# Transformer and state-space layers on one core: the tree layer's preparation moved from step 11 to step 17 of the second attention loop, and four kinds of DVE work in the first loop a step later

## The chip, the cores and the metric

The kernel runs on one core of a Trainium2 chip. The metric is the device time of one execution in microseconds (us), lower is better. Engines are named as in the profile: PE (TensorE), DVE (VectorE), ACT (ScalarE), POOL (GpSimd) and SP (SyncE), which only issues DMAs here.

## The reference

Six layers are applied in turn to x, four batches of 512 tokens by 128 features, each with its own layer norm:

```
x = x + 0.5 * ffn(layernorm(x))      # three decision trees of 16 leaves make q, k, v; full attention
x = x + mha(layernorm(x))            # 16 heads of 8, rotary positions, ALiBi, causal softmax
x = x + 0.5 * ffn(layernorm(x))
x = x + 0.5 * moe(layernorm(x))      # 8 experts, the best 2 of each token, and a shared one
x = x + mamba(layernorm(x))          # convolution, then a scan over 16 states
x = x + 0.5 * moe(layernorm(x))
```

Only the attention layer and the preparation of the tree layer behind it are touched. Their cores:

```
q = rope(x @ wq.T); k = rope(x @ wk.T); v = x @ wv.T          # 16 heads of 8
scores = q @ k.T / sqrt(8) + slope_h * (j - i), causal
out = softmax(scores) @ v @ out_w.T + out_b
...
for _ in range(4):                                            # the path through one tree
    score = xf . node_w[cur] + node_b[cur]; cur = 2*cur + 1 + (score >= 0)
```

## The kernel before

The four batches are worked through as two **pairs**. Within a pair each layer is two **units**, one for each batch (slot 0 and slot 1), so there are 24 units in all. Every engine runs its own program, written out by hand in the order in which it is to work; engines wait for each other by semaphores. Nothing is scheduled by a compiler: what stands behind a waiting instruction on an engine waits too.

A unit begins with a **prologue**: statistics of x ("stats"), the reciprocal root on POOL and three small DVE steps, then the normed rows ("rows"), a transposition on PE ("turn"), the high part on ACT ("high"), the low part on DVE ("low"). For a tree unit the paths follow: a product with the nodes' weights ("first"), then three times a count on PE and a comparison on DVE ("second", "third", "fourth"). For an attention unit four projections on PE and their rotation on DVE follow ("first", "second" for the queries, "k first", "k second" for the keys); the rotated rows are then split into three bf16 parts. ACT copies a part ("q 0" to "q 2", "k 0" to "k 2", line L920), DVE subtracts it (line L1432), which leaves the rest for the next part. The DVE stages of the rests have the names "third", "fourth", "k rest", "k last". When the last part of a side is there, SP writes the parts to DRAM in six DMAs (`head_rows`, L622) and loads them back spread over the heads (`head_rows_in`, L629 for queries, L633 for keys).

The prologue of a unit is **hosted** in the loop of the unit ahead of it, one stage in a step, so that it fills gaps. Tables say which stage falls in which step, for each engine. `stage_at` (L138) reads them, and `HEAD_LAG` says by how many steps the host's counter is shifted: in the attention loop stage number n comes at step n + HEAD_LAG[slot].

The **attention loop** of a unit (`mha`, on every engine) has 32 steps, 8 for each quad of four heads. In a step PE makes the scores of two heads for a tile of keys (L1790, masks L1793 or L1795) and ACT takes the exponentials (L1011); PE needs those of two steps before to go on, since the scores have two places in PSUM. Every other step PE multiplies with the values (L1819). For numerical safety each query row's maximum must be known before its scores are made. That is the work of the **slots**: a small score product on PE (L1858, mask L1860) and a maximum on DVE (L1446). There are 11 slots for a quad. When a quad's slots are done, DVE splits the maxima into parts (L1453 to L1456), PE transposes them (job "turn", L1573 from a_mp), ACT copies them out (L1028), SP writes and reloads them (L721, L725). `HEADS_PLAN` says which of these jobs fall in which step. The slots of the second unit start in step 19 of the first one's loop, behind "turn" 3, and end in step 17 of the second's. Other jobs: "rows" (PE transposes a quad's result from a_o, DVE normalises it: L1411, L1412), "vals" (the values, ACT copy L1034), "ctr" and "out" (the output projection). The jobs share two PSUM banks by turns: PE may start a job only when the job two places before it in the list has been read out of its bank (`bank_free`). In a step an engine does the loop's own work first, then the jobs of that step, and the hosted stage last.

The first unit's loop hosts the prologue of the second attention unit. In steps 4 to 13 fall the splits and the key rotations; their DVE steps are 4, 5, 6, 8, 11 and 12, and ACT copies its parts in steps 4, 5, 6, 11, 12 and 13. The second unit's loop hosts the tree unit's prologue.

The first slot of the second unit needs the keys loaded back (`rows_of_quads`):

```
1823            def rows_of_quads(k, n):
1825                pe.wait_ge(a_fill.sem, a_fill.at(k // 2, 1 if n < 2 else 3))
1826                pe.wait_ge(a_ldq[n].sem, a_ldq[n].at(k, 0))
1827                pe.wait_ge(a_ldk[n].sem, a_ldk[n].at(k, 1))
```

On ACT a part waits for the rest before it, on DVE a rest waits for its part:

```
 914                        act.wait_ge(a_res.sem, a_res.at(k, 2 * side + c - 1))
1431                dve.wait_ge(a_prt.sem, a_prt.at(k, 3 * side + c))
```

Of the kernel before, what the change touches and what calls it, by code (L numbers as in the profile page):

```python
# [51 lines left out]
def heads_plan():  # L52
# [13 lines left out]
    for step in range(2 * NS2):  # L66
# [15 lines left out]
        if step == NS2 + 9:  # L82
# [15 lines left out]
DVE_STAGES = {0: "stats", 2: "rows", 6: "low", 8: "first", 10: "second", 12: "third",  # L98
              14: "fourth", 15: "ranks", 16: "combine", 17: "row"}
# [31 lines left out]
HEAD_PARTS = [f"{side} {c}" for side in "qk" for c in range(3)]  # L131
HEAD_ROTATIONS = ["first", "second", "k first", "k second"]
HEAD_RESIDUALS = ["third", "fourth", "k rest", "k last"]
HEAD_LAG = {0: -6, 1: 11}
KEYS_LATER = 2


def stage_at(table, i, kind, host):  # L138

    if kind == "mha" and table is not POOL_STAGES:  # L140
        for own, ahead in ((DVE_STAGES, HEAD_DVE_STAGES), (ACT_STAGES, HEAD_ACT_STAGES), (PE_STAGES, HEAD_PE_STAGES)):
            if table is own:
                if host == "mha":
                    ahead = {n + KEYS_LATER * (n >= 15): name for n, name in ahead.items()}
                    if table is ACT_STAGES:
                        ahead[3] = "norm"
                return ahead.get(i)
    if host == "mamba" and table is ACT_STAGES:
        return LOOP_ACT_STAGES[kind].get(i)
    if host == "mamba" and kind == "moe" and table is not POOL_STAGES:  # L150
        return {"stats": LOOP_DVE_STAGES, "turn": LOOP_PE_STAGES}[table[min(table)]].get(i)
    if kind == "mamba":
        table = {n: name for n, name in table.items() if name in ("stats", "guess", "rows", "turn", "high", "low")}
    return table.get(i)
# [25 lines left out]
def program(nc, A, out):  # L180
    with ExitStack() as ctx:
# [579 lines left out]
        def _(pool):  # L761
# [31 lines left out]
            def hand_over(u, i):  # L793
                if u + 1 < NU:
                    prologue(u + 1, stage_at(POOL_STAGES, i, UNITS[u + 1][0], UNITS[u][0]))
# [66 lines left out]
        def _(act):  # L862
# [135 lines left out]
            def mha(u, k):  # L998
# [6 lines left out]
                for s_ in range(NS2):  # L1005
# [8 lines left out]
                    for job, x, n in HEADS_PLAN[at]:  # L1014
                        head_job(k - p + x, job, n)
                    if s_ >= HEAD_LAG[p] + 5 and s_ >= 1:
                        hand_over(u, s_ - HEAD_LAG[p])
                if p == 1:
                    heads_out(k - 1, 2 * QUADS - 1)

            def head_job(k, job, n):
                b = job_bank(HEADS_JOBS.index((job, k % 2, n)))
                if job == "turn":
                    act.wait_ge(a_mtr.sem, a_mtr.at(k, n))
                    if n >= 1 or k % 2 == 1:

                        act.wait_ge(a_mwr.sem, a_mwr.at(k, n - 1))
                    a_mok.by(act.activation(a_mT, bank[0:12, b, 0:T // 2].bitcast(BF16), ACT.Copy))  # L1028
                if job == "vals":
                    act.wait_ge(a_vpr.sem, a_vpr.at(k, 0))  # L1030
                    if k % 2 == 1:

                        act.wait_ge(a_vok.sem, a_vok.at(k - 1, 1))
                    a_vst.by(act.activation(flat(a_vs[:]), bank[:, b, :], ACT.Copy))  # L1034
                if job == "ctr":
                    act.wait_ge(a_ctr.sem, a_ctr.at(k, 0))
                    a_cok.by(act.activation(a_o[:], bank[:, b, :], ACT.Copy))
# [73 lines left out]
            def hand_over(u, i):  # L1111
                if u + 1 < NU:
                    prologue(u + 1, stage_at(ACT_STAGES, i, UNITS[u + 1][0], UNITS[u][0]))
# [13 lines left out]
        def _(dve):  # L1127
# [257 lines left out]
            def mha(u, k, p):  # L1385
# [11 lines left out]
                for s_ in range(NS2):  # L1397
                    for job, x, which in HEADS_PLAN[NS2 * p + s_]:
                        head_job(k - p + x, job, which, b - p + x)
                    if s_ >= HEAD_LAG[p] and s_ >= 1:  # L1400
                        hand_over(u, s_ - HEAD_LAG[p])
            def normalise(k, g):

                dve.wait_ge(a_otr.sem, a_otr.at(k, g))
                if g >= 1 or k % 2 == 1:
                    dve.wait_ge(a_norm.sem, a_norm.at(k, g - 1))
                if g == 0 and k % 2 == 1:

                    dve.wait_ge(a_ctr.sem, a_ctr.at(k - 1, 0))
                src = bank[:, job_bank(HEADS_JOBS.index(("rows", k % 2, g))), :].rearrange("p (t c w) -> p t c w", t=NT, c=4)  # L1410
                step(V.reciprocal(a_rec[:], src[:, :, :, DH]))  # L1411
                a_norm.by(V.tensor_tensor(a_rows[:, :, 32 * g:32 * g + 32].rearrange("p t (c d) -> p t c d", d=DH),  # L1412
                                          src[:, :, :, 0:DH], a_rec[:].unsqueeze(3).to_broadcast([P, NT, 4, DH]),
                                          ALU.mult))
# [19 lines left out]
            def head_job(k, job, n, batch):  # L1434
                if job == "rows":
                    normalise(k, n)
                if job == "out":
                    dve.wait_ge(a_out.sem, a_out.at(k, 0))
                    a_fin.by(add_rows(batch, bank[:, job_bank(HEADS_JOBS.index((job, k % 2, n))), :]))
                    dve.wait_ge(a_fin.sem, a_fin.at(k, 0))  # L1440
                if job == "slot":
                    quad, (qt, h0, nh) = n // NS1, SLOTS_4[n % NS1]
                    w = (qt + 1) * P
                    dve.wait_ge(a_s1.sem, a_s1.at(k, n))
                    src = bank[:, job_bank(HEADS_JOBS.index((job, k % 2, n))), 0:nh * w].rearrange("p (h w) -> p h w", w=w)
                    a_m1.by(V.tensor_reduce(a_mx[:, quad, qt, h0:h0 + nh], src, AX_X, ALU.max, negate=True))  # L1446
                    if n % NS1 == NS1 - 1:
                        max_parts(k, quad)
# [96 lines left out]
            def hand_over(u, i):  # L1545
                if u + 1 < NU:
                    prologue(u + 1, stage_at(DVE_STAGES, i, UNITS[u + 1][0], UNITS[u][0]))
# [10 lines left out]
        def _(pe):  # L1558
# [208 lines left out]
            def mha(u, k, p):  # L1767
# [9 lines left out]
                for s_ in range(NS2 + 3 * p):  # L1777
# [23 lines left out]
                    if at >= 3 and at % 2 == 1:  # L1801
                        weigh_heads(k - p, (at - 3) // 2)
                    if s_ > HEAD_LAG[p] and 1 <= s_ < NS2:
                        hand_over(u, s_ - HEAD_LAG[p])
            def weigh_heads(k, tile):

                quad, kt = divmod(tile, NT)
                x, g = divmod(quad, QUADS)
                pe.wait_ge(a_e2.sem, a_e2.at(k, 2 * tile + 1))
                if kt == 0 and quad >= 1:  # L1810
                    pe.wait_ge(a_osb.sem, a_osb.at(k, quad - 1))
                if tile == 0:
                    pe.wait_ge(a_fill.sem, a_fill.at(k // 2, 4))
                if kt == 0 and g in (0, 3):

                    pe.wait_ge(a_vok.sem, a_vok.at(k + x, g // 3))
                for c in range(4):
                    ring = (2 * tile + c // 2) % 4
                    ins = mm(bank[32 * c:32 * c + 32, 6, kt * P:T], a_v[:, kt, 4 * g + c, :],  # L1819
                             a_p[:, ring, c % 2, 0:T - kt * P], start=kt == 0, stop=kt == NT - 1)  # L1820
                a_pv.by(ins)
# [175 lines left out]
            def hand_over(u, i):  # L1997
                if u + 1 < NU:
                    prologue(u + 1, stage_at(PE_STAGES, i, UNITS[u + 1][0], UNITS[u][0]))
# [143 lines left out]
```

## Time and profile before

| | |
|---|---|
| median of 3 runs | 1291.39 us (1291.34 to 1293.13) |
| the profiled execution, its own time | 1288.87 us |
| its span in the profile | 1287.1 us |
| PE busy | 1218.5 us, 95% |
| DVE busy | 898.2 us, 70% |
| ACT busy | 643.6 us, 50% |
| POOL busy | 241.6 us, 19% |
| granted TensorE clock, mean | 0.999 |

The span runs from the first to the last instruction that the profiler saw; the execution's own time has 1.8 us around it. The busy shares are means over very different stages. In the timelines below a row is a group of equal instructions: start, length, engine, line, output and inputs, and in brackets how long the engine had been idle before it and which instruction ended that.

### The profile page before, as it was taken

How to read it: one execution, taken by the hardware profiler on the slowest of the kernel's cores; microseconds unless marked ns; L12 is line 12 of the kernel's file. 1: busy time of each engine (PE TensorE's matmuls, PEld its weight loads, DVE VectorE, ACT ScalarE, POOL GpSimd, SP SyncE). 2: the span in 40 equal slices, each digit the busy share in tenths (PEclk: the TensorE clock that was granted, in tenths of full speed). 3: DMA queues.
4: the chain of work that ended last, by engine and by line, in shares of the span. 5: the costliest groups of instructions: out<-in, count | busy, mean ns of one | idle time of the engine just before them, and what ended most of it. 6: DMA issues, size and time to landing. Idle time of an engine off the chain costs nothing.

```text
span 1287.1 us, 17292 instructions
## 1 busy us (share of the span) xinstructions
PE 1218.5 (95%) x6158; PEld 781.7 (61%) x6158; DVE 898.2 (70%) x1732; ACT 643.6 (50%) x1196; POOL 241.6 (19%) x205
## 2 busy tenths in 40 slices
PE   6999888999999999899999988989999999999998
PEld 3676444567666555566667754446776664555665
DVE  7756867455666798986764677655465768989765
ACT  4544555443422697942234445453443228979222
POOL 3001000000020093842000010000000204938210
PEclk9999999999999999999999999999999999999999
DMA  7203130000101121220100032200002102121110
GB/s 237 60 31 97 46 84 12 1 1 1 66 1 66 47 95 37 92 80 1 75 25 1 25 91 69 52 3 1 1 1 66 67 1 76 66 76 66 67 74 8
DMA packets 34069, 63.27 MB, mean 49 GB/s; under 512 B 4576, under 2 KB 20288, under 8 KB 33792
## 3 DMA queue, kind: packets, MB, share of 16 engines
q1 hardware_dynamic: 33984, 62.17, 15.5%
q8 instruction: 49, 0.80, 0.3%
q14 instruction: 36, 0.29, 0.1%
HBM read 54.23 MB, written 8.45 MB: 49 GB/s over the span
## 4 chain that ended last, share of the span: by engine, by line
PE 71%; DVE 14%; ACT 7%; issue 4%; POOL 2%; DMA 2%; SPq 1%; DVEq 0%; ACTq 0%; POOLq 0%
PE bank L1564 13%; PE bank L1566 13%; PE bank L1565 13%; PE bank L1750 10%; PE bank L1573 4%; DVE a_mx L1446 4%; PE bank L1909 3%; PE bank L1643 3%; PE bank L1717 2%; PE bank L1819 2%; POOL n_hc L855 2%; ACT n_part L1108 2%; DVE n_h L1534 2%; PE bank L1790 2%; ACT n_da L1100 2%
## 5 line engine op out<-in xcount | busy, mean ns | idle before, releaser
L1290 DVE SCALAR_TENSOR_TENSOR f_hl<-bank,f_hh 128x512 fp32r<-128x512 f32 x192 | 131.6, 688 | 124.2 <-ACT f_hh L930 122.9
L993 ACT ACTIVATE m_sl<-bank 128x512 f32<-128x512 f32 x144 | 86.0, 599 | 235.3 <-PE bank L1566 231.6
L930 ACT ACTIVATE f_hh<-bank 128x512 fp32r<-128x512 f32 x192 | 114.7, 597 | 168.2 <-PE bank L1643 168.0
L855 POOL TENSOR_TENSOR n_hc<-n_h,n_cs 128x512 f32<-128x512 f32 x128 | 160.6, 1283 | 34.0 <-DVE n_h L1534 30.0
L1564 PE MATMUL bank<-xT_h,mw_h 128*128 128x512 f32 x288 | 160.5, 557 | 2.1 <-DVE m_h L1367 1.7
L1534 DVE TENSOR_TENSOR_SCAN n_h<-n_da,bank 128x512 f32<-128x512 f32 x128 | 149.0, 1204 | 4.2 <-PE bank L1573 1.3
L1750 PE MATMUL bank<-m_h,mw 128*128 128x512 f32 x288 | 145.5, 594 | 0.0
L1357 DVE TENSOR_TENSOR m_t<-m_sl,bank 128x512 f32<-128x512 f32 x128 | 87.8, 686 | 78.2 <-PE bank L1566 77.1
L786 POOL TENSOR_TENSOR small<-small,half 128x4 f32<-128x4 f32 (+1 forms) x24 | 26.8, 1116 | 556.0 <-DVE small L1193 556.0
L1909 PE MATMUL bank<-n_hc,ident 128*128 128x512 f32 x256 | 130.1, 596 | 0.2
L1446 DVE TENSOR_REDUCE a_mx<-bank 128x1 f32<-128x384 f32 (+3 forms) x176 | 105.8, 637 | 31.0 <-PE bank L1860 28.7
L1011 ACT ACTIVATE a_p<-bank 128x1024 f32<-128x1024 f32 (+3 forms) x128 | 87.8, 704 | 78.7 <-PE bank L1795 42.0
L1566 PE MATMUL bank<-xT_h,mw_l 128*128 128x512 f32 x288 | 114.0, 396 | 0.0
L1565 PE MATMUL bank<-xT_l,mw_h 128*128 128x512 f32 x288 | 113.5, 394 | 0.0
L1564 PE MATMUL bank<-f_hh,fw_h 128*128 128x512 f32 x192 | 109.6, 571 | 0.0
L1573 PEld LDWEIGHTS bank<-ident,n_part 128*128 128x128 f32 x480 | 55.8, 140 | 76.8 <-issue 45.4
L1108 ACT ACTIVATE n_part<-bank,n_bT 128x256 f32<-128x256 f32 x240 | 97.3, 548 | 0.9 <-PE bank L1573 0.7
L1100 ACT ACTIVATE n_da<-n_dt,amat 128x512 f32<-128x512 f32 x128 | 91.0, 791 | 4.9 <-DVE n_h L1534 3.3
L1573 PE MATMUL bank<-ident,n_part 128*128 128x128 f32 x480 | 73.2, 277 | 13.9 <-ACT n_part L1108 7.6
L1564 PE MATMUL bank<-xT_h,fw_h 128*128 128x512 f32 x192 | 83.5, 435 | 0.9 <-DVE R L1222 0.9
L1365 DVE TENSOR_TENSOR m_h<-m_t,m_c 128x512 f32<-128x512 f32 x112 | 77.4, 691 | 4.5 <-DMA m_c<-comb_dram 0.6
L1858 PE MATMUL bank<-a_k,a_q 128*128 128x128 bf16 (+3 forms) x256 | 63.8, 302 | 14.9 <-DVE a_mx L1446 12.5
(248 smaller groups left out, 2339.5 us busy)
## 6 DMA issues: line engine op xcount, KB each, us to landing
n_cs<-c_dram SPq DMA_DIRECT2D x32, 512.0 KB, 3.7
m_c<-comb_dram SPq DMA_DIRECT2D x28, 512.0 KB, 5.2
a_q<-stack_dram SPq DMA_DIRECT2D x16, 256.0 KB, 3.8
a_k<-stack_dram SPq DMA_DIRECT2D x32, 128.0 KB, 3.6
stage_fw<-in_fw_dram SPq DMA_DIRECT2D x6, 512.0 KB, 7.3
stack_dram<-R SPq DMA_DIRECT2D x16, 192.0 KB, 2.8
w_stage<-in_mw_dram SPq DMA_DIRECT2D x9, 256.0 KB, 2.7
stack_dram<-R SPq DMA_DIRECT2D x16, 128.0 KB, 2.7
```

Source lines behind the costliest of these rows:

```text
L855: n_hcs.by(nc.gpsimd.tensor_tensor(n_hc[:, i % 4, :], n_h[:, i % 4, :], n_cs[:, j % C_RING, i // 2 % 2, :], ALU.mult))
L1100: n_das.by(act.activation(n_da[:, i % 4, :], n_dt[:, i % 2, :], ACT.Exp, scale=amat[:, i % 2, i // 2:i // 2 + 1]))
L1108: ins = act.activation(n_sx[p][:, n % 2, c, :], dtx_rows(c), ACT.Copy, scale=n_bT[:, c, n:n + 1])
L1290: f_lo.by(V.scalar_tensor_tensor(f_h[1][:, i % 4, :], bank[:, i % 3, :], 0.0, f_h[0][:, i % 4, :].bitcast(F32), ALU.max, ALU.subtract))
L1446: a_m1.by(V.tensor_reduce(a_mx[:, quad, qt, h0:h0 + nh], src, AX_X, ALU.max, negate=True))
L1534: n_scan.by(V.tensor_tensor_scan(n_h[:, i % 4, :], n_da[:, i % 4, :], drive(i), 0.0, ALU.mult, ALU.add))
L1564: mm(dst, w[0], x[0], start=start, stop=False)
L1565: mm(dst, w[0], x[1], start=False, stop=False)
L1566: return mm(dst, w[1], x[0], start=False, stop=stop)
L1573: ins = nc.tensor.transpose(dst(t), src(t), idn)
L1750: m_s2.by(mm(bank[:, 6, :], mw2[:, e, m, :], m_h[:, i2 % 3, :], start=i2 == 0, stop=i2 == MSTEPS - 1))
L1909: n_ya.by(mm(bank[:, 2 + i % 2, :], ident[:], n_hc[:, i % 4, :], start=i < 2, stop=i >= 2 * NSTATE - 2))
```

## The change

Two numbers of the hand-written order change; no instruction is added or removed, and the order on SP and POOL is the same.

```
-HEAD_LAG = {0: -6, 1: 11}
+HEAD_LAG = {0: -6, 1: 17}
...
                     if table is ACT_STAGES:
                         ahead[3] = "norm"
+                    if table is DVE_STAGES:
+                        ahead = {n + (n >= 10): name for n, name in ahead.items()}
                 return ahead.get(i)
```

The first edit moves the tree unit's prologue, on PE, DVE and ACT, six steps later in the second attention unit's loop: DVE's "stats" from step 11 to step 17, "rows" from 13 to 19, PE's "turn" from 15 to 21, ACT's "high" from 16 to 22, and so on to DVE's "fourth" from 25 to 31. The second edit moves DVE's stages "third", "fourth", "k first", "k second", "k rest" and "k last" of the second attention unit from steps 4, 5, 6, 8, 11, 12 of the first unit's loop to steps 5, 6, 7, 9, 12, 13. PE's and ACT's stages of that prologue stay where they are. Both edits act once in each pair. The change adds two lines, so that lines behind L147 have numbers higher by 2 in it.

DVE's order in the first unit's loop, steps 9 to 14, before. L1423 and L1427 are the rotation "k second", L1432 the rests "k rest" and "k last", L1446 the maxima of slots, L1411 and L1412 the job "rows":

```order
L1423 SCALAR_TENSOR_TENSOR xn<-bank,rope 128x512
L1427 TENSOR_TENSOR xn<-xn 128x512
L1446 TENSOR_REDUCE a_mx<-bank 128x1 x3
L1453 CAST a_mp<-a_mx 128x4x4
L1454 TENSOR_TENSOR a_mr<-a_mx,a_mp 128x16
L1455 TENSOR_TENSOR a_mp<-a_mx,a_mp 128x4x4
L1456 TENSOR_TENSOR a_mp<-a_mr,a_mp 128x4x4
L1446 TENSOR_REDUCE a_mx<-bank 128x4
L1446 TENSOR_REDUCE a_mx<-bank 128x2
L1432 TENSOR_TENSOR xn<-xn,R 128x512 x2
L1446 TENSOR_REDUCE a_mx<-bank 128x2
L1446 TENSOR_REDUCE a_mx<-bank 128x1
```

The same place in the change:

```order
L1425 SCALAR_TENSOR_TENSOR xn<-bank,rope 128x512
L1429 TENSOR_TENSOR xn<-xn 128x512
L1448 TENSOR_REDUCE a_mx<-bank 128x1
...
L1448 TENSOR_REDUCE a_mx<-bank 128x4
L1448 TENSOR_REDUCE a_mx<-bank 128x2
L1434 TENSOR_TENSOR xn<-xn,R 128x512
L1448 TENSOR_REDUCE a_mx<-bank 128x2
L1448 TENSOR_REDUCE a_mx<-bank 128x1
L1413 RECIPROCAL a_rec<-bank 128x16
L1414 TENSOR_TENSOR R<-bank,a_rec 128x4x32
L1434 TENSOR_TENSOR xn<-xn,R 128x512
L1448 TENSOR_REDUCE a_mx<-bank 128x1 x7
```

The rotation "k second" moved behind two maxima that it stood ahead of, and "k last" moved behind the two maxima of step 13 and the job "rows".

DVE's order in the second unit's loop, steps 11 to 19, before. L1174 to L1193 are "stats", L1168 to L1206 "rows":

```order
L1174 BN_STATS st<-X 128x6 x4
L1177 BN_AGGR mv<-st 128x2 x4
L1193 TENSOR_SCALAR small<-mv 128x4
L1446 TENSOR_REDUCE a_mx<-bank 128x2
L1446 TENSOR_REDUCE a_mx<-bank 128x1 x2
L1411 RECIPROCAL a_rec<-bank 128x16
L1412 TENSOR_TENSOR R<-bank,a_rec 128x4x32
L1168 SCALAR_TENSOR_TENSOR small<-small 128x4
...
L1206 TENSOR_SCALAR xn<-X,mv,small 128x128 x4
L1446 TENSOR_REDUCE a_mx<-bank 128x1 x6
L1453 CAST a_mp<-a_mx 128x4x4
```

In the change:

```order
L1448 TENSOR_REDUCE a_mx<-bank 128x1 x6
L1455 CAST a_mp<-a_mx 128x4x4
L1456 TENSOR_TENSOR a_mr<-a_mx,a_mp 128x16
L1457 TENSOR_TENSOR a_mp<-a_mx,a_mp 128x4x4
L1458 TENSOR_TENSOR a_mp<-a_mr,a_mp 128x4x4
L1176 BN_STATS st<-X 128x6 x4
L1179 BN_AGGR mv<-st 128x2 x4
L1195 TENSOR_SCALAR small<-mv 128x4
L1170 SCALAR_TENSOR_TENSOR small<-small 128x4
...
L1208 TENSOR_SCALAR xn<-X,mv,small 128x128 x4
L1413 RECIPROCAL a_rec<-bank 128x16
```

Both stages of the prologue moved behind the last maximum and its parts.

## Rows read from the trace of the kernel before

**Rows 1.** The page: the chain that ended last, share of the span by engine.

```profile
PE 71%; DVE 14%; ACT 7%; issue 4%; POOL 2%; DMA 2%; SPq 1%; DVEq 0%; ACTq 0%; POOLq 0%
```

**Rows 2.** Stretches of both loops, first pair: engines busy us (instructions), clock, DMA.

```profile
138.40:191.90 53.50, 47.21 (x397) 23.66 (x394) 38.69 (x80) 29.45 (x47) 0.51 (x1) 1.00 0.24 63
191.90:237.20 45.30, 40.68 (x362) 20.11 (x358) 27.18 (x69) 25.84 (x41) 1.30 (x2) 1.00 0.05 13
```

**Rows 3.** The chain that ended last, 161 to 174 us: start, us, what.

```profile
161.78 0.63 ACT R L920
...
162.44 0.70 DVE xn L1432
...
163.16 0.64 ACT R L920
...
163.82 0.64 SPq L622
...
167.14 2.08 DMA stack_dram<-R
...
169.24 0.63 SPq L633
...
169.91 3.07 DMA a_k<-stack_dram
```

**Rows 4.** PE's timeline at the second unit's first slot, both pairs.

```profile
173.12 0.38 PE L1858 MATMUL bank<-a_k,a_q 128*128 128x128 bf16 x4 [0.45 <-DMA a_k<-stack_dram]
...
805.14 0.38 PE L1858 MATMUL bank<-a_k,a_q 128*128 128x128 bf16 x4 [0.57 <-DMA a_k<-stack_dram]
```

**Rows 5.** PE's timeline in the first unit's loop.

```profile
149.91 0.34 PE L1858 MATMUL bank<-a_k,a_q 128*128 128x384 bf16 x1 [0.57 <-DVE a_mx L1446]
...
163.78 0.66 PE L1573 MATMUL bank<-ident,a_o 128*128 128x128 f32 x4 [1.45 <-DVE a_mx L1446]
...
172.28 0.38 PE L1573 MATMUL bank<-cbf,a_mp 128*12 128x128 bf16 x4 [1.15 <-DVE a_mp L1456]
```

**Rows 6.** DVE's timeline in the first unit's loop.

```profile
148.56 0.69 DVE L1432 TENSOR_TENSOR xn<-xn,R 128x512 f32<-128x512 f32 x1 [0.69 <-ACT R L920]
...
155.55 1.91 DVE L1446 TENSOR_REDUCE a_mx<-bank 128x1 f32<-128x512 f32 x3
...
163.05 1.15 DVE L1446 TENSOR_REDUCE a_mx<-bank 128x2 f32<-128x512 f32 x2
164.48 0.26 DVE L1411 RECIPROCAL a_rec<-bank 128x16 f32<-128x16 f32 x1 [0.28 <-PE bank L1573]
164.77 0.29 DVE L1412 TENSOR_TENSOR R<-bank,a_rec 128x128 f32<-128x128 f32 x1
```

**Rows 7.** DVE's timeline: a loop part without hosted work, then the tree unit's stages.

```profile
187.18 1.74 DVE L1446 TENSOR_REDUCE a_mx<-bank 128x2 f32<-128x512 f32 x3 [1.49 <-PE bank L1860]
...
210.47 0.86 DVE L1174 BATCH_NORM_STATS2 st<-X 128x6 f32<-128x128 f32 x4
...
214.95 1.12 DVE L1206 TENSOR_SCALAR xn<-X,mv,small 128x128 f32<-128x128 f32 x4
```

**Rows 8.** PE's timeline: the same slot without and with hosted work, then later waits.

```profile
191.02 0.39 PE L1858 MATMUL bank<-a_k,a_q 128*128 128x512 bf16 x1 [0.21 <-DVE a_mx L1446]
...
216.59 0.39 PE L1858 MATMUL bank<-a_k,a_q 128*128 128x512 bf16 x1 [0.99 <-DVE a_mx L1446]
...
227.65 0.39 PE L1599 MATMUL bank<-dbit,tree 96*128 96x512 bf16 x1 [0.23 <-DVE R L1222]
...
232.75 1.07 PE L1819 MATMUL bank<-a_p,a_v 128*32 128x512 f32 x8 [0.63 <-ACT a_p L1011]
```

**Rows 9.** POOL's timeline: the reciprocal root of the tree unit's prologue.

```profile
212.03 1.01 POOL L786 TENSOR_TENSOR small<-small,half 128x4 f32<-128x4 f32 x1 [17.10 <-DVE small L1193]
```

**Rows 10.** PE's timeline at the kernel's start: one kind of matmul, early and later.

```profile
17.84 0.63 PE L1565 MATMUL bank<-xT_l,fw_h 128*128 128x512 f32 x1
...
20.92 0.40 PE L1565 MATMUL bank<-f_hl,fw_h 128*128 128x512 f32 x1
```

## The prediction

> **What bounds the kernel now.** I read the page first, then the two stretches that the change touches, then the chain of waits in them, and last the timelines of PE, DVE and ACT step by step. The chain that ended last lies on PE for 71% and on DVE for 14% [rows 1], so PE sets the end, with DVE's answers in between. In the first unit's loop PE is busy 47.21 of 53.50 us, in the second's 40.68 of 45.30 [rows 2]; the rest is waits, and only they can change, since no instruction is added or removed. Both pairs show the same picture 632.01 us apart, so every term counts twice.
>
> In the first loop the chain leaves PE for a long stretch [rows 3]: ACT copies "k 1" (161.78), DVE subtracts it ("k last", 162.44), ACT copies "k 2" (163.16, 0.64), and in the same moment SP begins its six writes (163.82). The last is issued at 167.14 and lands 2.08 us later; the keys are loaded, the second load is issued at 169.91 and lands after 3.07. PE then begins the second unit's first slot at 173.12 and had waited 0.45 for that load, in the second pair 0.57 [rows 4]. So the end of "k 2" at 163.80 has no slack: a microsecond later there is a microsecond at PE's slot, since the same six writes and loads hang on it in a fixed order.
>
> **The first unit's loop, DVE a step later.** What it gives first. DVE sat idle 0.69 us for ACT's copy before "third" [rows 6], and PE waited 0.57 for a slot's bank behind it [rows 5]. Now DVE takes the two maxima of step 5 first, and "third" finds its copy ready. PE's wait of 0.57 goes. The price is that ACT now waits at "q 1" for a subtraction of its own step, some 0.4 us, with exponentials that PE needs only two steps later; that cover holds, as "q 2" then starts within 0.2 us of its old time.
>
> At steps 9 and 10 there is a loss. "k second", two operations of 0.69, stands behind the maxima of step 9 and ahead of that of step 10. Before, the three maxima ran in one piece (155.55, 1.91 long, [rows 6]) and ended at 157.46. Now DVE has 30 and 31 done at about 155.7, the two rotations at 157.1, and slot 32 at 157.7. A slot of step 11 waits for this bank, so PE is there some 0.2 us later than before.
>
> At step 13 the long wait of PE, 1.45 us at 163.78 [rows 5], was for the first of two maxima (163.05 [rows 6]) which stood behind "k last", itself behind ACT. DVE now does it as soon as PE's slot is there, and is done at about 162.9; PE transposes at 162.95, 0.8 earlier than before.
>
> But "k last" now stands behind both maxima and the job "rows". Its new time: transposition 162.95 + 0.66 [rows 5] = 163.6; reciprocal and product, 164.48 to 165.06 before [rows 6], take 0.58 and a gap, so 164.2; "k last" 0.70 and a gap, 164.9; "k 2" 0.64, **165.5 in place of 163.8, 1.7 us later** [rows 3]. SP, which has nothing else left to issue by then, waits too. Writes, landing and loads are the same, so the slot of 173.12 comes at 174.8. All that PE gained before is lost there: it would reach that slot at about 172.3 (the transposition of "turn" 3, 172.28 after a wait of 1.15 [rows 5], moves forward by 0.8) and stands still for 3 us.
>
> The bounds of this term: if PE's transposition did not come forward at all, "rows" would end at 165.06 as before [rows 6], and 0.70 and 0.64 behind it give 166.4, so +2.6. If the loss of 0.2 at step 11 did not occur, the transposition would come 0.3 earlier, so +1.4. Taken: **+1.7 a pair**. The max rows of "turn" 3 lie behind the loads on SP and are wanted only in the next quad; they were held up by ACT before and move back less than the slot does.
>
> **The second unit's loop, the prologue six steps later.** "stats" costs PE nothing at its old place: DVE idles 1.49 us at the same place of a quad without it [rows 7], and "stats", from 210.47 [rows 7] to POOL's start at 212.03 [rows 9], is as long. "rows" is another matter: with three small steps of 0.2 each ahead (an estimate from the reciprocal's 0.26 [rows 6]) and the normed rows (214.95, 1.12 [rows 7]) it lies between maxima, and PE's next slot waits 0.99 instead of 0.21 [rows 8]. Moved behind the last maximum this goes: **-0.78**.
>
> PE's own hosted work (transposition, product, three counts: about 1.9 us) moves unchanged, worth nothing in itself. The waits around it change. At the new place there are no maxima, PE's steps are short, and the prologue's chain is tight. I laid the old durations end to end in the new order. PE's step 16 then begins 1.3 us earlier, at 216.75 (0.78, and the transposition that left): parts of the maxima done 220.6, "stats" to 222.0, POOL's root 1.01 [rows 9] to 223.1, "rows" 1.7 to 224.85; PE is at "turn" at 224.6 and waits 0.3. ACT's "high" stands behind an exponential of the same step and ends at 226.7, DVE's "low" at 227.4; PE wants to begin "first" at 227.05 and waits 0.45. Two small ones follow (0.15 for ACT, 0.35 for the comparison before "fourth", which stands behind DVE's "rows" job), and the wait for a_o in the last quad (0.63 [rows 8]) stays. Gone are the old waits at the counts and products (0.23 at 227.65 [rows 8], and about 0.6 in shorter ones at two other places, an estimate). The sum: new 1.25, old 0.85 and 0.78; with 0.1 that overlaps, **about -0.5 a pair**. Bounds: all new waits hidden and the one of 0.63 too gives -2.0; all as computed and nothing won at 216.59, 0.
>
> **Sum.** 2 x (1.7 - 0.5) = +2.4 us. The profiled execution took 1288.87, so one like it would take 1291.3; against the median of the runs, 1291.39, which lies 2.5 higher, the forecast is **1293.8 us**. 0.2% of the time, which is about what a measurement of this kernel can tell from no change, is 2.6 us, so this forecast lies just inside.
>
> **A rule that speaks against the change.** The first row to look at is what PE does after a stop. Between the slot's two neighbours PE would be idle for 3 us, longer than any wait in these loops before (1.45 [rows 5]). At the kernel's start, with PE idle until 8.4 us and then waiting often, a matmul of 512 columns took 0.63 us, later the same kind 0.40 [rows 10]; in both loops the granted clock is 1.00 [rows 2], the upper of its two levels, 2.4 GHz. The Trainium skill's page "TensorE: Matmul & The Clock Gate", section "HAM oscillation — how this bites in real kernels", says that waits of PE for transfers can drop its clock to half, so that the work after each begins slowly. By that rule the sum would be larger than by the rows, which show no drop after waits of 1.45.
>
> **Rivals.** (a) *The load is not the limit, and the kernel gets faster.* The decisive point is whether PE still waits for a_k at the second unit's first slot. If the six writes and the loads took 1.7 us less than before, or "k last" were reached by 163.1, PE would keep its 0.8 and the two loops would give 2 x (-0.8 - 0.5) = -2.6, so 1288.8. For it: PE's waits of 0.57 and 1.45 do go. Against it: rows 3 and 4, with a wait on the load in both pairs, and DVE's order, which has "k last" behind four operations that need PE. Chance 0.10.
>
> (b) *The second loop gives nothing*, because the late "turn" and "high" hold PE more than computed (a chain over five engines with PE's steps so short; each hand-over may slip a step). Then 2 x 1.7 = 3.4, with the bound of 2.6 up to 5.2: 1295 to 1296.6, middle 1295.5. Chance 0.15.
>
> (c) *PE's clock falls after the wait of 3 us.* Price from rows: the slow and the quick matmul of the start are 3.1 us apart and 0.63 and 0.40 long [rows 10]; 3.1 x (1 - 0.40 / 0.63) is 1.1 us a pair, 2.3 in all: 1296.1. The skill's page names this case. Against it: 3 us is not much more than what passes here without a drop. Chance 0.07.
>
> (d) *The second loop gives all it can*, -2.0 a pair, and the first costs 1.7: -0.6 in all, 1290.8. It needs ACT's wait of 0.63 to go too, for which nothing speaks. Chance 0.08.
>
> **How the numbers follow.** The forecast has 0.60; its own spread, from the bounds of both terms, is about 1291.5 to 1296, of which 0.34 lies within 2.6 us and 0.26 above. Within 0.2%: 0.34 and (d) 0.08, and 0.02 of (a), is 0.44. Slower: 0.26, (b) 0.15 and (c) 0.07 is 0.48. Faster: 0.08 of (a). That the two sides are this close comes from the size of the sum, not from doubt about its sign. The range leaves out most of (a) and the upper end of (b): 1290.5 to 1297.0.
>
> **What would show it.** In the changed kernel's chain of waits ACT's last L922 before the six writes ends at about 165.5 (L920 before), the writes start right behind, and PE's product at the second unit's first slot (L1860, L1858 before) has an idle time of about 3 us before it, ended by a DMA of a_k. The first loop (138.4 to the second unit's first scores at 191.9) is about 55.2 us long instead of 53.5. PE's waits of 0.57 at 149.9 and 1.45 at 163.8 are gone or short. In the second loop the slot that waited 0.99 waits 0.2, the transposition of xn and the product "first" have waits of 0.3 to 0.5, and the loop is about 44.8 us long instead of 45.3. The forecast is wrong if the slot's wait for a_k is under 1 us, if "k last" runs before the job "rows" is done, or if the second loop is longer than before.

## The result and the profile after

| | before | the change |
|---|---|---|
| median of 9 runs each | 1291.39 us (1289.51 to 1293.13) | 1296.35 us (1295.00 to 1297.23, one run left out) |
| ratio to before, 95% interval | | 1.0036 (1.0026 to 1.0047) |
| the profiled execution | 1288.87 us, span 1287.1 | 1296.35 us, span 1294.6 |
| PE busy | 1218.5 us | 1222.6 us |
| granted TensorE clock, mean | 0.999 | 0.996 |

The change is slower, by 4.96 us between the medians. The forecast was 1293.8 (+2.4), so the sign and the range hold, and the size does not. One of the nine runs of the change was disturbed (2036.62 us); 1296.35 is the median with it, 1296.17 (+4.8) without, and such runs are left out of every ratio and range below. PE runs the same instructions and yet is busy 4.1 us longer; that is the first hint that not only waits grew.

In the changed kernel line numbers behind L147 are higher by 2. Its page has the chain by engine of [rows 1] within one point each, and one slice of the clock line, the sixth of 40 (162 to 194 us), is not at full clock:

```profile
PE 1222.6 (94%) x6158; PEld 783.4 (61%) x6158; DVE 898.8 (69%) x1732; ACT 644.5 (50%) x1196; POOL 241.5 (19%) x205
...
PEclk9999989999999999999999999999999999999999
...
PE 71%; DVE 14%; ACT 6%; issue 4%; POOL 3%; DMA 2%; SPq 1%; DVEq 0%; POOLq 0%; ACTq 0%
```

The chain of waits in the first unit's loop, answering [rows 3] (start, us, what). It now goes from PE over DVE's slot maximum, the job "rows" and "k last" (L1434) to "k 2" (L922), the writes and the loads:

```profile
162.45 0.70 DVE a_mx L1448
163.16 0.04 issue
163.20 0.67 PE bank L1575 x4
163.87 0.02 issue
163.89 0.27 DVE a_rec L1413
164.16 0.02 issue
164.19 0.29 DVE R L1414
164.48 0.61 DVE xn L1434
165.09 0.02 issue
165.11 0.64 ACT R L922
165.75 0.02 issue
165.76 0.64 SPq L624
...
169.08 2.08 DMA stack_dram<-R
...
171.18 0.63 SPq L635
...
171.85 3.50 DMA a_k<-stack_dram
```

PE's timeline, answering [rows 4, 5]. The waits of 0.57 and 1.45 have gone or shrunk to 0.38, two others (0.54 for reloaded maxima, 0.99) have come, and in both pairs PE stands still for over 3 us at the second unit's first slot:

```profile
152.13 0.39 PE L1792 MATMUL bank<-a_q,a_k 128*128 128x512 bf16 x1 [0.54 <-DMA a_q<-max_dram]
...
158.01 0.39 PE L1860 MATMUL bank<-a_k,a_q 128*128 128x256 bf16 x2 [0.99 <-DVE a_mx L1448]
...
171.71 0.38 PE L1575 MATMUL bank<-cbf,a_mp 128*12 128x128 bf16 x4 [1.15 <-DVE a_mp L1458]
175.49 0.59 PE L1860 MATMUL bank<-a_k,a_q 128*128 128x128 bf16 x4 [3.39 <-DMA a_k<-stack_dram]
...
177.07 1.94 PE L1821 MATMUL bank<-a_p,a_v 128*32 128x512 f32 x8
...
196.79 0.39 PE L1792 MATMUL bank<-a_q,a_k 128*128 128x512 bf16 x1
...
220.64 0.39 PE L1860 MATMUL bank<-a_k,a_q 128*128 128x512 bf16 x1 [0.21 <-DVE a_mx L1448]
...
811.53 0.38 PE L1860 MATMUL bank<-a_k,a_q 128*128 128x128 bf16 x4 [3.30 <-DMA a_k<-stack_dram]
...
812.44 1.94 PE L1821 MATMUL bank<-a_p,a_v 128*32 128x512 f32 x8
```

The wait of 3.39 does not stand alone: 1.15 us of idle time lie just ahead of it, with 0.38 us of work between (171.71), so PE works 0.38 us in over 4.9. The four matmuls of the slot took 0.38 us before [rows 4]. In pair 1 they take 0.59 now; in pair 2 they still take 0.38, and the slow matmuls begin behind them. The product with the values (L1821) is slow in both pairs and took 1.07 before:

```profile
173.98 1.07 PE L1819 MATMUL bank<-a_p,a_v 128*32 128x512 f32 x8
```

The stretches around that slot in the changed kernel (columns: stretch, its length, busy us and instructions of PE, PEld, DVE, ACT and POOL, granted clock, DMA share, GB/s). The clock is 1.00, falls to 0.50 during the wait and is back at 1.00 from about 181 us. The last row is from pair 2, where the clock fell at 812.3, 0.7 us after PE had begun to work again, and was back at about 815.7:

```profile
171.00:174.00 3.00, 0.38 (x4) 0.23 (x4) 0.50 (x4) 1.48 (x3) 0.00 (x0) 1.00 0.64 158
174.00:176.00 2.00, 0.51 (x5) 0.54 (x6) 0.00 (x0) 0.00 (x0) 0.00 (x0) 0.50 0.87 226
176.00:179.00 3.00, 3.00 (x14) 0.59 (x13) 1.33 (x2) 0.00 (x0) 0.00 (x0) 0.50 0.21 46
179.00:181.00 2.00, 2.00 (x12) 1.37 (x11) 0.56 (x1) 0.60 (x1) 0.00 (x0) 0.55 0.02 6
181.00:184.00 3.00, 2.72 (x25) 1.38 (x24) 1.82 (x6) 0.94 (x2) 0.00 (x0) 1.00 0.00 0
...
812.00:816.00 4.00, 4.00 (x22) 1.64 (x21) 1.49 (x3) 0.60 (x1) 0.00 (x0) 0.57 0.15 42
```

**Where the time of the profiled execution went**, by the same instruction in both traces. In pair 1 the slot comes 2.37 us later (173.12, now 175.49). The second unit's first scores, which stood at 191.97, come at 196.79: 4.82 later, so another 2.45 went between the slot and them, where PE ran at the lower clock. The tree unit's first product comes at 241.47 instead of 237.23, 4.24 later, so the second loop gave 0.58 back. In pair 2 the three numbers are 2.03, 1.56 and 0.57, net 3.02. The two pairs make 7.26 of the 7.5 us by which the spans differ.

The profiled execution of the kernel before was one of its quicker ones, 2.5 us under its median, which is why the two profiles stand 7.5 us apart and the medians 4.96. What fills those 2.5 us is looked into below.

### The profile page after: what moved, and what is told of

Its sections match the earlier page's. It is cut to its first block, busy times and chain, and to the rows that moved or that the text cites. A ratio compares the mean times of both kernels' runs of the same rounds, so it can differ in the third digit from the quotient of the medians.

```text
span 1294.6 us, 17292 instructions
## 1 busy us (share of the span) xinstructions
PE 1222.6 (94%) x6158; PEld 783.4 (61%) x6158; DVE 898.8 (69%) x1732; ACT 644.5 (50%) x1196; POOL 241.5 (19%) x205
## 4 chain that ended last, share of the span: by engine, by line
PE 71%; DVE 14%; ACT 6%; issue 4%; POOL 3%; DMA 2%; SPq 1%; DVEq 0%; POOLq 0%; ACTq 0%
PE bank L1566 13%; PE bank L1568 13%; PE bank L1567 13%; PE bank L1752 10%; PE bank L1575 4%; DVE a_mx L1448 4%; PE bank L1911 3%; PE bank L1645 3%; POOL n_hc L857 2%; PE bank L1719 2%; PE bank L1821 2%; DVE n_h L1536 2%; ACT n_part L1110 2%; PE bank L1792 2%; ACT n_da L1102 1%
```

## The experiments

Every run has its ratio to the kernel before on the same chip in the same session, with a 95% interval. The names of edits: "the first edit" is the tree unit's prologue six steps later, "the second edit" DVE's stages a step later.

**The two edits apart.** `e1_loop2_only` has the first edit alone:

```
-HEAD_LAG = {0: -6, 1: 11}
+HEAD_LAG = {0: -6, 1: 17}
```

> Only the first edit: the tree unit's prologue from step 17, DVE's stages of the first loop as before. Theory (the loss is all in the first loop): the first loop stays as before, 53.5 us, and the second gets 0.6 us shorter a pair as in the changed kernel (4.88 us late at its start, 4.24 at its end), so about 1.3 us under the kernel before, no clock drop. Rival (the late prologue is itself part of the loss): at or above the kernel before.

Measured: 1288.18 us (1287.85 to 1290.13), ratio 0.9987 (0.9978 to 0.9996). It left no trace that can be read, so the same kernel was run again later:

> The first edit alone once more, on the same chip as the other two and for a profile of its second loop. Theory: a median of 1288.2 to 1289, above that of e9 by the clock drops of some executions; PE's slot at step 15 of the second loop waits 0.21 instead of 0.99.

Measured: 1289.64 us (1287.9 to 1291.47), ratio 0.9991 (0.9983 to 1.0). Together the first edit by itself is a gain of 1 to 2 us.

`e2_loop1_only` has the second edit alone:

```
+                    if table is DVE_STAGES:
+                        ahead = {n + (n >= 10): name for n, name in ahead.items()}
```

> Only the second edit: DVE's six stages a step later, the tree unit's prologue from step 11. Theory: the whole loss, 4.9 us a pair in the profile, at PE's wait for the keys and in the slow matmuls behind it; so slower than the change by about 1.3 us, and 6 us above the kernel before. Rival (the two edits add up otherwise): less loss than the change shows.

Measured: 1296.09 us (1295.78 to 1296.48), ratio 1.0048 (1.0034 to 1.0062). The second edit holds the whole loss. It was expected to be 1.3 us slower than the change, for want of the first edit's gain; by the ratios it is 1.5 us slower, which their intervals don't separate from nothing. PE's timeline of this kernel shows the wait with its slow matmuls behind it, and the second loop's old wait:

```profile
175.13 0.59 PE L1860 MATMUL bank<-a_k,a_q 128*128 128x128 bf16 x4 [3.27 <-DMA a_k<-stack_dram]
...
220.56 0.39 PE L1860 MATMUL bank<-a_k,a_q 128*128 128x512 bf16 x1 [0.99 <-DVE a_mx L1448]
```

**Which stage.** The rival to "k last behind the job rows" is that the key rotations or the other rests cost it. `e8_k_last_only` shifts "k last" alone, without the first edit:

```
+                    if table is DVE_STAGES:
+                        ahead = {n + (n >= 18): name for n, name in ahead.items()}
```

> The kernel before with one stage moved: k last from step 12 to step 13 of the first loop. Theory (this one move holds the loss): the six writes begin at about 165.5 instead of 163.8, PE waits about 3 us or more for a_k at the second unit's first slot, the clock falls there, and the time is 5 to 6 us above the kernel before although PE's wait of 1.45 shrinks. Rival (it needs the other stages too, which put the rotation in the way): under 2 us above.

Measured: 1296.48 us (1295.89 to 1297.29), ratio 1.0046 (1.0033 to 1.0059), the same loss as e2 with one stage of six moved. Its PE timeline:

```profile
162.78 0.66 PE L1575 MATMUL bank<-ident,a_o 128*128 128x128 f32 x4 [0.38 <-DVE a_mx L1448]
...
175.01 0.58 PE L1860 MATMUL bank<-a_k,a_q 128*128 128x128 bf16 x4 [3.34 <-DMA a_k<-stack_dram]
```

`e3_k_rests_back` is the change with "k rest" and "k last" back at their old steps:

```
-                        ahead = {n + (n >= 10): name for n, name in ahead.items()}
+                        ahead = {n + (10 <= n < 17): name for n, name in ahead.items()}
```

> The change, but the stages k rest and k last stay in their old steps 11 and 12; third, fourth, k first and k second are a step later. Theory (k last behind two maxima and the job rows delays the copy k 2 and with it the six writes): the writes begin at about 164.3 instead of 165.76 (163.82 before), late only by the 0.5 us that k second costs at step 11; PE's wait for a_k is 1.5 us or less, no clock drop; the time is within 1 us of the kernel before. Rival (k second behind the maxima is what delays the writes): they begin near 165.7 all the same and the time stays at 1296.

Measured: 1289.07 us (1288.62 to 1290.51), ratio 0.9995 (0.9986 to 1.0003). The writes begin at 164.20, the first slot's wait is 0.74 in pair 1 and 0.83 in pair 2, and the old wait of 1.45 is back. One part of the expectation failed: the clock did fall in pair 2 of the profiled execution, behind the slot of 805.67 (0.75 on the mean from 805 to 808 us), with no wait of over 1.45 us near it. PE's timeline:

```profile
157.90 0.39 PE L1860 MATMUL bank<-a_k,a_q 128*128 128x256 bf16 x2 [0.99 <-DVE a_mx L1448]
...
164.17 0.66 PE L1575 MATMUL bank<-ident,a_o 128*128 128x128 f32 x4 [1.45 <-DVE a_mx L1448]
...
805.67 0.38 PE L1860 MATMUL bank<-a_k,a_q 128*128 128x128 bf16 x4 [0.83 <-DMA a_k<-stack_dram]
```

Its other wait, the 0.99 at 157.90, belongs to "k second". `e5_k_second_back` has that rotation back at its old step as well:

```
-                        ahead = {n + (n >= 10): name for n, name in ahead.items()}
+                        ahead = {n + (10 <= n < 14): name for n, name in ahead.items()}
```

> The change, but k second, k rest and k last stay at their old steps; third, fourth and k first are a step later. Theory: the 0.5 us that PE lost at step 11 are not lost, the writes begin at 163.8 or a little before, and what third and fourth give PE at step 6 is lost again at the wait for the reloaded maxima at step 8; so as with the first edit alone, 1288.2. Rival (the moved first stages give something that lasts): under 1287.5.

Measured: 1288.96 us (1288.01 to 1291.34), ratio 0.9989 (0.998 to 0.9997). It can't be told from the first edit alone: the stages "third", "fourth" and "k first" a step later give and cost nothing that these runs resolve. In the first pair of its profiled execution the clock fell, and not at a wait of 3 us but at the one of 1.45 that the kernel before has too. The four transpositions behind it, 0.66 us elsewhere, took 0.98, and the clock of the stretch was 0.79. PE's timeline, then the stretches:

```profile
163.73 0.98 PE L1575 MATMUL bank<-ident,a_o 128*128 128x128 f32 x4 [1.45 <-DVE a_mx L1448]
```

```profile
164.00:172.00 8.00, 7.79 (x60) 3.57 (x60) 4.25 (x9) 2.88 (x5) 0.00 (x0) 0.79 0.63 161
```

**The price of the clock.** `e4_pe_busy` is the change with 18 idle matmuls of 384 columns, into a bank that nobody reads then, ahead of the second unit's first slot. The wait for the keys stays; PE only isn't idle in it:

```
                         for job, x, which in HEADS_PLAN[at]:
+                            if (job, x, which) == ("slot", 1, 0):
+                                keep_busy(18, 7)
                             head_job(k - p + x, job, which)
```

> The change, with 18 idle matmuls of 384 columns into an unused bank ahead of PE's wait for the second unit's first slot. They take about 3 us of the 3.4 that PE waits. Theory (the clock falls because PE stands still, and the slow matmuls cost 2.5 us a pair): the granted clock stays 1.00 in both loops, the wait itself stays as long, and the kernel gets 5 us faster than the change, to about 1291. Rival (the slowness after the wait is the DMAs', not the clock's): no gain, 1296.

Measured: 1292.13 us (1291.0 to 1292.75), ratio 1.0014 (1.0005 to 1.0023), 4.2 us under the change's median, with PE given more to do. The two medians are from different sessions, in which the kernel before had 1290.51 and 1291.39; by the two ratios the gain is 2.8 us, and that is the number to use. The mean clock of all its 11 runs is 0.999 or 1.000, where the change's lie from 0.994 to 0.997. The slot comes as late as in the change (175.35 against 175.49), but behind it the matmuls have their old durations. The second unit's first scores come at 194.20, 2.23 us later than in the kernel before, which is just what the slot is late (175.35 against 173.12). So nothing is lost between the slot and them, where the change lost 2.45. That shows the clock, and not the DMAs, as the cause of that part:

```profile
171.91 3.10 PE L1899 MATMUL bank<-cbf 128*128 128x384 bf16 x18
175.35 0.38 PE L1862 MATMUL bank<-a_k,a_q 128*128 128x128 bf16 x4 [0.34 <-DMA a_k<-stack_dram]
...
176.21 1.07 PE L1823 MATMUL bank<-a_p,a_v 128*32 128x512 f32 x8
...
194.20 0.39 PE L1792 MATMUL bank<-a_q,a_k 128*128 128x512 bf16 x1
```

**Earlier writes.** If the keys' writes are what is late, those that need only an early part can be issued before "k last". In `e6_early_writes_change` (the change) and `e7_early_writes_loop2` (the first edit alone) SP issues the two writes that hold only part 0 of the keys in the quad before, then the two that hold parts 0 and 1, and last the two that hold all three, so that two writes stand behind "k 2" instead of six:

```
-            def head_rows(k, side):
+            def head_rows(k, side, runs=((0, 2), (1, 2), (2, 2))):
...
-                for slot, n, part in PART_RUNS:
+                for run, needs in runs:
+                    slot, n, part = PART_RUNS[run]
+                    sp.wait_ge(a_prt.sem, a_prt.at(k, 3 * side + needs))
...
-                        if p == 0 and quad in (1, 2):
-                            head_rows(k + 1, quad - 1)
+                        if p == 0 and quad == 1:
+                            head_rows(k + 1, 0)
+                            head_rows(k + 1, 1, ((2, 0),))
+                        if p == 0 and quad == 2:
+                            head_rows(k + 1, 1, ((1, 1), (0, 2)))
```

> The change, with the six writes of the keys in the opposite order: the two that need only part 0 are issued when that is there, the two that need part 1 when that is, and only two wait for k 2. Theory (the writes' place behind k 2 sets PE's wait): the last write is issued at about 166.4 instead of 169.1, the keys land near 172.7, PE's wait of 3.4 us shrinks to about 0.7, the clock falls seldom or not, and the time is 1287 to 1288. Rival (the loads' landing is limited by the DMA engines, not by when the writes are issued): a wait of 2 us and more stays and the time is over 1292.

Measured: 1290.88 us (1288.74 to 1293.68), ratio 1.0002 (0.9992 to 1.0012). SP's queue in e6 (L729 reloads the maxima, L626 writes the parts), then PE's timeline of it in both pairs:

```profile
163.30 1.53 SPq L729 DMA_DIRECT2D a_q<-max_dram  x2
...
165.20 2.62 SPq L626 DMA_DIRECT2D stack_dram<-R  x4
...
170.21 1.26 SPq L637 DMA_DIRECT2D a_k<-stack_dram  x2
```

```profile
174.39 0.38 PE L1865 MATMUL bank<-a_k,a_q 128*128 128x128 bf16 x4 [2.19 <-DMA a_k<-stack_dram]
...
807.42 0.59 PE L1865 MATMUL bank<-a_k,a_q 128*128 128x128 bf16 x4 [1.37 <-DMA a_k<-stack_dram]
```

The first keys' load is issued at 170.21 instead of 171.18, and PE's wait falls from 3.39 to 2.19. That took most of the loss away, which shows that the writes behind "k 2" carry it. It was less than expected for two reasons. First, SP issued the two writes of part 1 no earlier than 165.20, though the part was there at 163.0 ("k 1" on ACT): it was held by the reload of the maxima, which began at 163.30 (162.44 in the change) and ended at 164.83. So the last write was issued at 167.20, where 166.4 was expected. Second, that write took 2.99 us from issue to landing, against 2.08 in the change: with the order turned round, the largest write (three parts) comes last, where the smallest (one part) did before.

> The first edit alone, with the writes as in e6. Theory: four writes stand behind k 2 at 163.8, the keys land about 1.3 us earlier, PE's wait for them (0.45) is gone and turn 3 sets the slot's time; 0.5 us a pair less than the first edit alone, so 1287.0, and hardly ever a clock drop. Rival (no time lies in the writes' order once k last is in step 12): 1288.2.

Measured: 1288.97 us (1287.94 to 1291.71), ratio 0.9989 (0.998 to 0.9997). A miss: nothing on top of the first edit that can be told. The slot's wait in pair 1 fell to 0.22, but in pair 2 it was 1.29, as long as in e11 without the early writes (1.34). SP's queue shows why the writes didn't come early there: "k 2" ended at 794.64, but SP stood in the reload of the maxima from 793.94 to 795.46 and issued the four writes that were left from 795.81 on. In e11 "k 2" ended at 795.34 and the writes began at 795.92, behind the reload as well. The writes of pair 2 hung on SP's reload and not on "k 2".

**Idle matmuls across the old waits.** `e9_loop2_busy` is the first edit alone with idle matmuls ahead of three jobs at which PE waits, `e10_before_busy` is the kernel before with the same line:

```
                         for job, x, which in HEADS_PLAN[at]:
+                            keep_busy({("rows", 0, 0): 8, ("turn", 0, 3): 6, ("slot", 1, 0): 2}.get((job, x, which), 0), 7)
                             head_job(k - p + x, job, which)
```

> The first edit alone, and in the first loop idle matmuls into an unused bank where PE waits: 8 ahead of its 1.45 us wait at step 13, 6 ahead of turn 3, 2 ahead of the second unit's first slot. Theory (the times of the first edit alone, 1287.85 to 1290.13, spread because the clock falls in some executions at these waits): no run has a drop, all lie within 0.5 us of 1287.9, and the second loop is about 0.6 us a pair shorter than before. Rival (the spread has another source): as wide a spread as without them.

Measured: 1288.25 us (1287.87 to 1288.86), ratio 0.9979 (0.997 to 0.9988): faster than both kernels.

> The kernel before with the same idle matmuls. Theory: the kernel before, which ran in 1289.0 to 1293.4, keeps to its lower end, 1289.1, for the same reason; the first edit is then worth 1.3 us against it. Rival: median unchanged at 1290.7.

Measured: 1289.37 us (1289.12 to 1291.15), ratio 0.9992 (0.9983 to 1.0002). PE's timeline in e9: the waits of 1.45, 1.15 and 0.45 have become 0.15, 0.18 and 0.29, at times (163.78, 172.29) that are those of [rows 5] within 0.01, so the idle matmuls fill the waits and delay nothing; the slot comes at 173.40, and at 173.42 in e11, which has none:

```profile
163.78 0.66 PE L1573 MATMUL bank<-ident,a_o 128*128 128x128 f32 x4 [0.15 <-DVE a_mx L1446]
...
170.98 1.14 PE L1896 MATMUL bank<-cbf 128*128 128x384 bf16 x6
172.29 0.38 PE L1573 MATMUL bank<-cbf,a_mp 128*12 128x128 bf16 x4 [0.18 <-DVE a_mp L1456]
...
173.40 0.38 PE L1859 MATMUL bank<-a_k,a_q 128*128 128x128 bf16 x4 [0.29 <-DMA a_k<-stack_dram]
```

In e10 one run took 1291.15 us with a mean clock of 0.999, so a long run without a lower clock occurs too, and its interval doesn't tell it from the kernel before.

These runs also tell how much of a median is clock. The mean clock of each run is known: of the 21 runs of the first edit alone (e1 and e11), those with 0.999 or 1.000 took 1287.85 to 1289.64 us, and those with 0.997 or 0.998 1289.46 to 1291.47. All 11 runs of e9 have 0.999 or 1.000 and none took over 1288.86. Of the 26 runs of the kernel before in the same session the seven with 0.999 or 1.000 took 1288.95 to 1290.96 us, the sixteen with 0.998 took 1290.23 to 1291.83, and the three with 0.997 took 1292.70 to 1293.42. So the spread of the kernel before goes with the clock too, and its profiled execution, with 0.999, was one in which the clock held.

## Why the prediction was right in sign and too small

| term of the prediction | forecast | measured |
|---|---|---|
| end of "k 2", pair 1 | 165.5 (+1.7) | 165.75 (+1.95) |
| the second unit's first slot, pair 1 | 174.8 (+1.7) | 175.49 (+2.37) |
| the same, pair 2, by the loop's own start | +1.7 | +2.03 |
| second loop, a pair | -0.5 | -0.58, -0.57 |
| both together, both pairs | +2.4 | +3.25 (2.37 + 2.03 - 1.15) |
| the clock, both pairs | 0 in the forecast, 2.3 in rival (c) | 4.01 (2.45 + 1.56) in the profile |

**The first loop went as computed, step by step.** "k last" stands behind the job "rows", "k 2" behind it, the six writes start with its end (165.76), and PE stands still for the load. All that PE gained before is lost at that slot. Expected were 3 us of standing still, 3.39 and 3.30 were seen. e8 shows that this one stage suffices and e3 that without the two rests the loss is gone; e6 shows that the writes behind "k 2" carry it on, since with four of the six taken out of that place most of it goes.

The size of +1.7 was low by 0.67 in pair 1, in two pieces. A slot at step 11 was to be 0.2 later for "k second", and PE waited 0.99 there and was 0.49 later (158.01 instead of 157.52). That puts 0.25 on "k 2" (165.75 instead of 165.5). The rest is the last load: 3.50 us from issue to landing instead of 3.07 [rows 3]. The forecast said "writes, landing and loads are the same"; the writes and their landing were (2.08 both times), the load wasn't; what made it longer no run shows. The bounds of +1.4 and +2.6 held it all.

A gain was also counted that did not arrive: the 0.57 at the slot of 149.91 [rows 5] turned into a wait of 0.54 two steps on, for the maxima reloaded by DMA (a_q from max_dram, at 152.13). The prediction followed the banks and ACT, not this load. It cost nothing in the end, because PE waits for the keys anyway.

**The second loop.** The slot that waited 0.99 [rows 8] waits 0.21 (220.64), "stats" and "rows" are off the busy steps, and new waits of 0.31 and 0.25 stand at the transposition and the product "first", where 0.3 and 0.45 were forecast:

```profile
225.58 0.38 PE L1575 MATMUL bank<-cbf,a_mp 128*12 128x128 bf16 x4 [0.87 <-DVE a_mp L1458]
229.79 0.66 PE L1575 MATMUL bank<-ident,xn 128*128 128x128 f32 x4 [0.31 <-DVE xn L1208]
232.35 0.47 PE L1566 MATMUL bank<-xT_h,rw_h 128*96 128x512 f32 x1 [0.25 <-DVE xT_l L1215]
236.20 1.06 PE L1821 MATMUL bank<-a_p,a_v 128*32 128x512 f32 x8 [0.63 <-ACT a_p L1013]
```

The wait of 0.63 in the last quad stays as forecast. The loop is 44.68 us long instead of 45.26. The cleanest measure of this edit is e9 against e10, which differ in it alone and have both a clock of 0.999 to 1.000: 1288.25 and 1289.37, so -1.12 for both pairs, where -1.0 was forecast. Rivals (b) and (d) fall, and (a) with them, since PE waits over 3 us for the keys.

**The step that failed** is the clock. The prediction had it as rival (c), with a chance of 0.07 and a price of 1.1 us a pair, and argued that "3 us is not much more than what passes here without a drop". Both parts were wrong. The clock fell to 0.50, the lower of its two levels (1.2 GHz), in both pairs of every execution of such a kernel that was profiled (the change, e2, e8). And the waits of 1.45 do not always pass without a drop: in e5 it fell at one of them. The forecast also took the 3 us as one wait by itself and left out the 1.15 us of idle time ahead of it. The price came from one slow matmul at the kernel's start over 3.1 us of work [rows 10]; in the loops PE runs 5.3 us of work at the lower level (175.49 to 180.82), and the same instructions took 2.85 us before (173.12 to 175.97). That is the 2.45 us of pair 1. Both parts of the price were low: the length (3.1 for 5.3) and the factor (0.63 / 0.40 is 1.6, while 5.33 / 2.85 is 1.9, since the listed lengths of neighbours overlap). In pair 2 the lower level lasted 3.4 us and cost 1.56.

The Trainium skill's page "TensorE: Matmul & The Clock Gate", section "HAM oscillation — how this bites in real kernels", says that PE's waits for transfers can halve its clock so that the work after each starts slowly. By that rule the trace agrees in pair 1, where the first matmuls behind the wait for the keys are slow (0.59 for 0.38); in pair 2 the clock fell only 0.7 us after work had begun. The prediction cited it and did not give it the weight.

How much of the result is which can be said from runs, by their ratios, since the sessions differ. Idle matmuls across the wait (e4) take the clock out of the change and leave the late keys: 1.0014. The kernel before with its own waits covered (e10) is at 0.9992. The difference, 0.0022 or 2.8 us, is the late keys less the second loop's gain, where the forecast's sum was +2.4 and the two profiles give 3.25. The clock takes another 0.0022 (2.8 us) from the change, whose interval and e4's don't overlap, and 0.0008 (1.0), which e10's interval doesn't tell from nothing, from the kernel before. So of the 4.6 us that the ratio of 1.0036 stands for, the mechanism that was forecast made about 2.8 and the clock the other 1.8 net, each good to about 1.5 us. The profiles put more on the clock (4.01), because the one of the kernel before was an execution in which it held.

The range held partly by luck. The late keys and the second loop alone, as measured, make 1294.2 to 1294.6; what carried the result to 1296.35 was a rival with a chance of 0.07, and the range reached that far mainly to take in the bounds of the first loop and rival (b).

**What stays open.** Whether the idle matmuls of e9 bring the median down or only its spread: its interval (0.997 to 0.9988) overlaps those of e1 and e11, the same kernel without them. That the clock fell in the longer executions of the kernel before rests on their mean clocks; no trace of one of them was kept. What decides whether it falls at a wait of 1.45 us or in a group of shorter ones is open too: it did in e5 (pair 1) and e3 (pair 2), and did not in the kernel before and e11.

## What to carry to other kernels

A stage that ends in a serial chain of DMAs (here six writes at 0.65 us each, a landing and a load) must be ranked by when its transfers are wanted, not by how idle its engine is: moved by one step it landed behind three hand-overs between PE and DVE, and a wait of 0.45 became 3.4. Before moving a stage, look for the wait whose releaser is a DMA and follow it back to the engine that starts it. And a wait on PE of a few microseconds has two prices, itself and the slow work behind it: if it can't be removed, idle matmuls into a free bank held the clock here (e4, e9) and delayed nothing, as they ended before what PE waited for. Waits that stand close together belong together when they are judged.

## What the hardware showed that was not expected

- The granted clock fell to 0.50 at a wait of 3.3 to 3.4 us (with one of 1.15 just ahead) inside a loop in which PE is otherwise busy for 88% of the time [rows 2]: in pair 1 during the wait, in pair 2 0.7 us behind it. It came back 5.3 and 4.2 us after work began again. A wait of 2.19 us (e6, pair 1) was followed by a fall as well, though only after the first matmuls behind it: the four of the slot took 0.38 as usual, and the clock of 176 to 182 us was 0.75. A wait of 1.45 us had one in e5 and none in the profiles of the kernel before and of e11. In pair 2 it fell at the slot in e6 behind waits of 1.15 and 1.37, and in e3 behind 1.15 and 0.83.
- Work at the lower level took up to 1.9 times as long: 5.33 us for 2.85 from the slot on, 1.94 for 1.07 in a product with the values. The loop lost 2.45 us in pair 1, with 5.3 us at that level, and 1.56 in pair 2, with 3.4, so a little under half of the time spent there.
- The larger a write, the longer it took from issue to landing in these loops: the medians in the change are 2.1 us for 64 KB (one part), 2.6 for 128 and 2.9 for 192 (three parts). So the order of the writes decides the landing of the last: 2.08 us in the change, 2.99 in e6. The keys' load took 3.07 us in the kernel before and 3.50 and 3.40 in the change and e6, with the same bytes; why it differs is not shown.
- 18 idle matmuls in the change's wait (e4) made the kernel 2.8 us faster by the ratios (4.2 by the medians), with 3.1 us more work on PE in each pair.
